# Routing in three blocks, fp8 rounding on later gate/up steps and slot arithmetic in the down phase of a fused attention and MoE kernel

## The reference

```python
x = x + fp8(layernorm(x)) @ fp8(ctx) + mask          # fp8: q = clip(x*scale, -448, 448).astype(float8_e4m3fn) / scale
h = layernorm(x)
scores = sigmoid(h @ router_w.T); sc = scores + e_bias            # 32 experts in 8 groups of 4
# the 3 best groups by their two best experts, then the 4 best experts in these groups
topk_w = scores[topk] / sum(scores[topk]) * 2.5
# each expert takes its first C = 160 slots, in token order
routed = scatter_add(slots, (silu(Xp @ W_gate) * (Xp @ W_up)) @ W_down * slot_weight)
x = x + routed + silu(h @ shared_gate.T) * (h @ shared_up.T) @ shared_down.T
```

## Time and profile before

| what | value |
|---|---|
| runs | 2235.83, 2236.72, 2240.79 us; median 2236.72 |
| profiled execution, span | 2236.8 us |
| busy | PE 1972.2 us (88%), DVE 1559.3 (70%), ACT 923.2 (41%), POOL 532.0 (24%) |
| chain that ended last | PE 71%, DVE 17%, issue 9% |
| mean granted TensorE clock | 0.976 of full speed |

### The profile page before, as it was taken

The page is one execution under the profiler, slowest core; times in us unless marked ns, Lnnn a source line. Parts: engine busy times, 40 slices in busy tenths (PEclk is TensorE's granted clock), DMA queues, the critical chain, the costliest instruction groups (busy, mean ns, idle before and its releaser), DMA issues.

```text
span 2236.8 us, 48554 instructions
## 1 busy us (share of the span) xinstructions
PE 1972.2 (88%) x19344; PEld 1618.5 (72%) x19344; DVE 1559.3 (70%) x2701; ACT 923.2 (41%) x1327; POOL 532.0 (24%) x560
## 2 busy tenths in 40 slices
PE   0016999999999999999999999979999999999997
PEld 0004576676667667667666766869999999999997
DVE  8998875675586576567546545458878888787884
ACT  4323321221221222122112121237777778777774
POOL 1011102112121210211212121124334343433432
PEclk9997999999999999999999999989999999999998
DMA  7734312112201211211110110379999999999993
GB/s 288 304 127 170 95 57 76 48 48 77 86 29 60 84 39 58 76 49 47 67 67 20 48 67 29 123 229 328 325 338 320 337 323 330 335 321 341 321 333 83
DMA packets 142356, 363.55 MB, mean 163 GB/s; under 512 B 18128, under 2 KB 18160, under 8 KB 142224
## 3 DMA queue, kind: packets, MB, share of 16 engines
q1 hardware_dynamic: 124656, 319.53, 40.5%
q0 software_dynamic: 16384, 42.03, 8.4%
q10 hardware_dynamic: 1184, 0.15, 0.0%
HBM read 306.37 MB, written 55.35 MB: 162 GB/s over the span
## 4 chain that ended last, share of the span: by engine, by line
PE 71%; DVE 17%; issue 9%; ACT 1%; POOL 1%; DMA 1%; ACTq 0%; SPq 0%; DVEq 0%; POOLq 0%
PE ps L1211 37%; PE ps L1222 13%; PE ps L1402 9%; PE ps L1249 4%; PE ps L1372 2%; DVE st L842 2%; PE ps L1351 2%; DVE amax L828 2%; DVE expo L241 1%; PE ps L1276 1%; PE ps L1294 1%; DVE W L925 1%; DVE SG L1081 1%; POOL slots L486 1%; DVE SG L1086 1%
## 5 line engine op out<-in xcount | busy, mean ns | idle before, releaser
L1211 PE MATMUL ps<-XT,W 128*128 128x256 f16 (+1 forms) x12288 | 1142.5, 255 | 59.0 <-DVE SG L1086 52.4
L1211 PEld LDWEIGHTS ps<-XT,W 128*128 128x128 f16 x12288 | 1031.8, 99 | 157.6 <-DVE SG L1086 58.5
L1149 DVE SCALAR_TENSOR_TENSOR W<-BIG,W 128x2048 f16<-128x2048 f32 x192 | 434.9, 2291 | 1.4 <-issue 1.4
L740 ACT ACTIVATE W<-BIG 128x2048 f16<-128x2048 f32 x192 | 365.1, 1904 | 0.0
L1222 PE MATMUL ps<-W,HH 128*128 128x512 f16 x1536 | 339.2, 379 | 1.7 <-DVE W L925 1.7
L1222 PEld LDWEIGHTS ps<-W,HH 128*128 128x128 f16 x1536 | 150.2, 98 | 176.3 <-DVE W L925 2.2
L1402 PE MATMUL ps<-HH,W 128*128 128x160 f16 x3072 | 217.9, 233 | 0.0
L241 POOL TENSOR_TENSOR expo<-expo 128x1 f32<-128x1 f32 x142 | 99.8, 703 | 485.9 <-ACT X L776 374.8
L1402 PEld LDWEIGHTS ps<-HH,W 128*128 128x128 f16 x3072 | 213.4, 98 | 0.2 <-DVE HH L1178 0.2
L687 ACT ACTIVATE HH<-SG 128x256 f16<-128x256 f32 x128 | 53.3, 417 | 379.7 <-DVE SG L1086 378.8
L1081 DVE SCALAR_TENSOR_TENSOR SG<-ps,SG 128x256 f32<-128x256 f32 x128 | 53.8, 421 | 212.2 <-ACT SG L682 212.2
(11 more groups left out here) (156 smaller groups left out, 2057.8 us busy)
## 6 DMA issues: line engine op xcount, KB each, us to landing
BIG<-in_w_gate SPq DMA_DIRECT2D x64, 1024.0 KB, 10.4
BIG<-in_w_up SPq DMA_DIRECT2D x64, 1024.0 KB
BIG<-in_w_down SPq DMA_DIRECT2D x64, 1024.0 KB
X<-in_x SPq DMA_DIRECT2D x16, 1024.0 KB, 5.0
xn_rows<-FR SPq DMA_DIRECT2D x32, 512.0 KB
out_rows<-X SPq DMA_DIRECT2D x32, 512.0 KB
W<-in_x SPq DMA_DIRECT2D x6, 2048.0 KB, 8.9
W<-in_ctx_in SPq DMA_DIRECT2D x6, 2048.0 KB, 7.8
```

Of the source, the lines that this page charges most:

```text
L740: ac.activation(dst, stage, ACT.Copy, scale=W_SCALE).then_inc(x_hi, 1)
L1149: ve.scalar_tensor_tensor(out=lo[cut], in0=src, scalar=W_SCALE, in1=hi[cut], op0=ALU.mult, op1=ALU.subtract).then_inc(x_lo, 1)
L1211: ins = te.matmul(out_ps, a[:, k, cols], b[:, k, :], start=n == 0, stop=n == len(steps) - 1)
```

## The change

`fp8_round` loses its clip. `route_picks` is cut into `route_groups` (the best groups, behind step 1), `route_experts` (the best experts, behind step 2) and `route_weights` (picks and weights, behind step 5; step 3 in the last group). The two `x_round` go from steps 2 and 3 to steps 3 and 4 (in group 0 from 3 and 4 to 4 and 5), the first `ctx_round` from step 4 to step 6 (in group 0 from 5 to 7). `route_slots` goes behind `shift(g + 1)`, ahead of the first `add_shared`. PE's five position matmuls go from behind step 5 to behind step 7, and their bank from 3 to 5, which down product u = 1 uses too: PE now waits for `d_route` of the same group ahead of u = 1. In the last group `route_slots` and the position matmuls stay where they are. With the clip gone, `fp8_round` writes the scratch in its first pass, so two waits for the rounding before are added.

```diff
-        pos_ps = PS[3][:, 64:64 + NT * E].rearrange("p (t e) -> p t e", t=NT)
+        pos_ps = PS[5][:, 0:NT * E].rearrange("p (t e) -> p t e", t=NT)
...
             def fp8_round(v, scratch, dst):
-                ch.link(ve.tensor_scalar(v, v, FP8_MAX, -FP8_MAX, ALU.min, ALU.max))
                 ch.link(ve.tensor_scalar(scratch.bitcast(I32), v.bitcast(I32), EXPONENT_BITS, None, ALU.bitwise_and))
...
                 wait(dve, pe_xq, 2 * f)
+                wait(dve, d_q, 2 * f + j)
                 fp8_round(xn[j], scratch, xq[j]).then_inc(d_q, 1)
...
             for m in range(4):
                 dve.wait_ge(a_cv, m + 1)
+                wait(dve, d_cq, 2 * m)
                 fp8_round(ctx0[m], M_first, BIG[:, 2 * m * D:2 * (m + 1) * D]).then_inc(d_cq, 2)
...
-            def route_picks(g):
+            def route_groups(g):
...
+            def route_experts():
...
+            def route_weights():
...
                     if ic == 1:
-                        route_picks(g)
-                    if front and ic - first in (2, 3):
-                        x_round(g + 1, ic - first - 2, M_main)
-                    if ctx and ic - first == 4:
+                        route_groups(g)
+                    if ic == 2:
+                        route_experts()
+                    if ic == (5 if front else 3):
+                        route_weights()
+                    if front and ic - first in (3, 4):
+                        x_round(g + 1, ic - first - 3, M_main)
+                    if ctx and ic - first == 6:
                         ctx_round(g, 2 * g + 9, 1, 2 * g + 10)
-                    if ic == 6:
+                    if ic == 6 and not front:
                         route_slots(g)
...
                 if front:
                     residual(g + 1, 1 - r)
                     shift(g + 1)
+                    route_slots(g)
...
                 wait(pe, a_lg, f)
-                wait(pe, d_route, f)
+                wait(pe, a_sc, f)
...
-                    if ic == 5:
+                    if front and ic == 6:
+                        xq_transpose(g + 1)
+                    if ic == (KS - 1 if front else 5):
                         pe.wait_ge(d_picks, g + 1)
-                        pe.wait_ge(a_sc, g + 1)
+                        wait(pe, d_out, 4 * g)
                         wait(pe, d_route, g)
...
-                    if front and ic == 6:
-                        xq_transpose(g + 1)
...
                     wait(pe, d_out, 4 * g + (u - 1 if u > 1 else 0))
+                    if u == 1:
+                        pe.wait_ge(d_route, g + 1)
...
-GROUP_STEPS = 62
+GROUP_STEPS = 58
```

More of the change, by code:

```diff
@@ L996, in route_picks @@
                 ch.sync()
+            def route_experts():
+                q = sc[:, :, :].rearrange("p t (g i) -> p (t g) i", i=EPG)
                 ch.link(ve.tensor_copy(g_idf[:, :, :], g_idx[:, :, :]))
```

## The result

The changed kernel takes 2179.14 us (median of 4 runs, 2178.33 to 2179.99) against 2237.3 (4 runs): a ratio of 0.974, with a 95% interval of 0.9726 to 0.9754. The prediction was 2175. The profiled execution has a span of 2176.9 us at a mean granted clock of 0.99.

The account below looks back on a forecast made before the run. PE was taken as the bound, held in places by DVE. Start -6.1, group 0 +2.2 and groups 1 to 14 -57.8 sum to -61.7 us, from 2236.8 to 2175; forecast 2168 to 2182 (0.72), 8 in 10 from 2166 to 2190.

Parts of the forecast that it names:

- The gap ahead of step 4: Gate/up steps: PE's 3.26 us wait while DVE does the whole routing; it goes, with 1.6 us to spare.
- the replay: Groups 1 to 14: DVE's pieces laid along PE's steps, leaving 0.7 to 5 us between DVE and PE.
- The floor of 74.95 us a group: Length of a group in which PE never waited: 80.05 - 5.10 us.
- The new gap at u = 1: Second down product: PE waits for route_slots, 0.65 us a group with the signal, all of it counting.
- rival 3: The new wait is hidden, and group 0 and the start do better: 2163 us; chance 0.07.
- The clock holds at the new gap: Down product u = 1: PE's clock does not fall at 0.65 us, a fifth of 3.26.
- rival 2: The clock falls at the new wait as at the old, 1.67 us a group: +23, 2198 us; chance 0.05.
- a clock under 1 in the down phase: Down phase: one of the signs in the profile after by which the prediction would be wrong.
- the 5.10 us between group 4 and group 15: Steps 2 to 5: 26.23 us in group 4 against 21.13 in group 15, put down to gap and low clock.
- The start: Ahead of group 0, driven by DVE: 6.1 us saved, clips 6.4 less three new waits of 0.1 each.
- 2.2 us lost: Group 0: residual where it starts today, route_slots' 2.25 us ahead of three splits; bounds -1.4 and +5.
- the one with 3.1: Group 0: if step 2's two products also wait for POOL's mask, step 4 starts at 222.8 and 3.1 us are lost.

Follow-up runs that it names:

- e7: Changed kernel with the three routing blocks put together again behind step 1: 2262.8 us, ratio 1.0088 to the kernel before.
- e3: Changed kernel with the position matmuls in bank 6 instead of 5, PE waiting for d_route behind u = 1: 2173.66 us, ratio 0.9702 to the kernel before.
- e5: Changed kernel with one more DVE pass of 1.23 us ahead of route_slots in groups 1 to 14: 2201.29 us, ratio 0.9826 to the kernel before.
- e6: Changed kernel with two more DVE passes ahead of route_slots in groups 1 to 14: 2232.92 us, ratio 0.9958 to the kernel before.
- e10: Changed kernel with the clip put back in fp8_round: 2192.83 us, ratio 0.9783 to the kernel before.
- e2: Changed kernel with the roundings one or two steps earlier, where they stood before: 2185.73 us, ratio 0.9747 to the kernel before.
- e1: Kernel before without the clip in fp8_round, with two waits for the rounding before, nothing moved: 2223.44 us, ratio 0.9916.
- e9: e3 with group 0's route_slots behind the three weight splits: 2170.7 us, ratio 0.9682 to the kernel before.
- e8: e9 with group 1's x_round at steps 3 and 4, and group 0's first ctx_round behind the first add_shared: 2164.59 us, ratio 0.9658 to the kernel before.
- e0: Kernel before, unchanged, profiled a second time: 2241.97 us, span 2240.0 us.

## Why the prediction was right, point by point

- **The gap ahead of step 4 is the routing's, and the cut takes it away**: right, shown by e7 from the other side. With the three blocks in one the gap is back at 3.3 us. Each hand-over of the replay that was looked up in group 3 came within 0.1 us.
- **The floor of 74.95 us a group**: right, shown by e3.
- **The new gap at u = 1**: right in place and size: it costs 0.64 to 0.81 us a group (waits of 0.48 to 0.65 and the 0.16) for 0.65, and e3 shows it to be all that stood above the floor. The groups gave 56.3 of the 57.8 us; the rest is that the first ones, which still round the context, wait 0.1 to 0.2 us longer and take 75.7 to 75.8 us, and 76.1 and 76.0 in groups 3 and 7 (in group 3 with 0.21 us of idle ahead of group 4 that the profile calls issue). For rival 3, the hidden gap, the prediction's own figures give 2162 and not 2163; it did not come.
- **The clock holds at the new gap**: right in groups 1 to 14; rival 2 is out at 0.6 us, and it did not fall behind e5's 1.8 us either. Behind e6's 3.1 us, at the same place, it did in seven of 14 groups. In group 0's down phase it did fall, behind 3.88 us: the prediction named a clock under 1 in the down phase as a sign that it is wrong, and for group 0 that sign came.
- **Edits costed at nothing in the groups** (the clip, the roundings' new steps): right in the new order (e10, e2: at most 0.5 us a group, or 5 us in all for the roundings). The prediction did not see that the old order had a second, smaller loss behind the gap, through the clip (e1). It changed nothing in the sum, because the 5.10 us between group 4 and group 15 held it already.
- **The start**: 5.9 for 6.1. Each new wait on the last pass costs 0.19 us and not 0.1 (the last pass of x starts 1.33 us ahead of the next rounding where it was 1.14), and there are four of them, not three: one between the two roundings of x and three between the four of the context. The trace does not agree here with the Trainium skill, VectorE: DVE Perf Modes, The DRAIN you can't avoid, by which a semaphore behind each instruction costs nothing extra.
- **Group 0 is where the sum failed**: "2.2 us lost" was 6.1 in this pair of profiles, and at least 3.8. The term named two things, a residual at the same time and route_slots' 2.25 us ahead of the splits; they came as 0.5 and 2.1 us. Not in it were two stretches at 1.2 GHz behind PE's waits of 2.75 and 3.88 us: the second half of the cross product at 5.30 us for 3.61, and the down product at 7.03 for 5.34, 3.4 us together. The prediction gave PE's late hand-overs their length only. The kernel before had a slow half too, as the fence below shows, but it was the first, ahead of the residual, which waited for DVE's queue anyway; in the changed kernel it is the half that the next residual and route_slots wait for. A third late hand-over that the prediction did not lay out, PE's wait of 5.57 us for the rounded x with step 7 at 7.56 us for 5.40 behind it, cost nothing up to the cross product: that starts 57.3 us behind the group's start, where before it started at 57.4, after 3.36 us of waiting for ACT. e9 shows the down product's part: with a wait of 1.7 us it takes 5.35 again. For the cross product e8 shows that the context rounding ahead of the residual held PE, and there the second half takes 3.61 us at full clock.
- **The sum came close partly by luck**: -59.9 for -61.7. The terms missed by +0.2 us (start), +3.9 (group 0), +1.5 (groups 1 to 14) and -3.8 (group 15 and experts). The last has no step in the prediction and hid two thirds of the others. On top of it the prediction took the span of 2236.8 us as a time, which, by the 1.9 us between the two in the other profiles, puts it that much low; the median is 4.1 us over 2175.
- **Beside POOL's mask in group 0**: the two products of the last fence below run wholly inside POOL's two additions (211.29 to 215.95) and take their usual 0.42 us each, while the comparison behind them (L1002), with both inputs in SBUF, takes 2.31 where it takes 0.21 in group 3. So the branch with 2.2 was the right one, not the one with 3.1: step 4 starts 26.85 us behind the group's start, for 26.65 in the prediction. The trace agrees with the Trainium skill, SBUF — State Buffer, Who interferes with whom, by which a Vector instruction with at most one input in SBUF, outside the two-port modes, does not contend with GpSimd, and one with two contends where GpSimd reads SBUF.
- **Group 15 and the experts** differ by 3.8 us with no step of the change in the experts, which make 3.7 of it; e0 and the other profiles have 759 to 761 us for the experts where these two had 758.3 and 754.6. The cause stays open.

The cross product of group 0 in the kernel before, first and second half (timeline of PE):

```profile
249.93 5.30 PE L1249 MATMUL ps<-BIG,FR 128*128 128x512 bf16 x16 [3.36 <-ACT FR L636]
255.71 3.61 PE L1249 MATMUL ps<-BIG,FR 128*128 128x512 bf16 x16 [0.48 <-DVE X L937]
```

Timelines of POOL and of DVE in group 0 of the changed kernel:

```profile
211.29 4.66 POOL L471 TENSOR_TENSOR X<-X,BIG 128x1024 f32<-128x1024 f32 x2 [31.66 <-ACT FR L626]
```

```profile
212.55 0.42 DVE L1087 SCALAR_TENSOR_TENSOR SG<-ps,SG 128x256 f32<-128x256 f32 x1 [5.48 <-ACT SG L682]
...
213.71 2.31 DVE L1002 TENSOR_TENSOR g_eq<-iota_e,g_idf 128x48 f32<-128x48 f32 x1
```

## What to carry to other kernels

Before costing a block of work that moves, write the hand-overs of one steady period along both engines, from the rows of the profile: here that gave the period to 0.1 us in 75.6, and named the next wait in advance. Treat the first period on its own and price each wait there with what the clock may lose behind it, since a period that carries extra work may have no slack for a moved block: the same edit cost 4 to 6 us in group 0. Where a shared PSUM bank forces a wait, look for one whose next writer comes later: that was worth 8.5 us. And add up the misses term by term before taking a close total as a confirmation.

## What the runs showed that I had not expected

- TensorE's clock behind a wait is not told by the wait's length alone: behind 3.1 us, at the same place of the same loop (e6), it fell to 1.2 GHz in seven of 14 groups; behind 3.3 us in four of 14 in e1, and in 13 of 14 in e7 (one of them behind 2.85 us), whose runs spread over 26 us. At the cross product of group 0 it fell behind 2.75 us in the changed kernel and in e9, where it had already fallen in the same group, behind 5.6 us, and not behind 2.76 in e8, where it had not. Behind 0.6 and 1.8 us it fell in none of 28.
- A fall cost 1.7 us behind each of the two waits in group 0, and up to 2.95 in e6, in products of 512 columns; in the gate/up steps of 256 columns it cost 1.67 in group 4 before and 2.8 in most groups of e7.
- The wait of DVE on its own last pass that the change adds costs 0.19 us.
